# A fused FFN / attention / FFN kernel: its first pass begins on rounded weights ahead of the branch on their low parts

## The reference

```
x = x + 0.5 * ffn(layernorm(x))
x = x + attention(layernorm(x))
x = x + 0.5 * ffn(layernorm(x))

ffn(x): h = silu(lin(x, w1)) * lin(x, w2)     # 256 -> 1024
        h = gelu(lin(h, h1))                  # 1024 -> 1024
        h = gelu(lin(h, h2))                  # 1024 -> 1024
        return lin(h, w3)                     # 1024 -> 256
lin(x, w) = (x @ w.T) * scale                 # w holds -1, 0, 1 in the given inputs
```

## Time and profile before

| | us |
|---|---|
| median of 3 runs | 1589.89 (1585.19 to 1591.61) |
| profiled execution | 1588.57 |
| its span, first to last instruction | 1586.7 |
| PE busy | 1498.8 |
| DVE busy | 1085.1 |
| ACT busy | 676.7 |
| POOL busy | 553.8 |
| mean DMA rate over the span | 216 GB/s |

### The profile page before, as it was taken

One profiled execution on the slowest core, in us unless ns is written; L12 is line 12 of the kernel. 1 busy time (PEld: TensorE's weight loads), 2 busy tenths in 40 slices (PEclk: granted clock), 3 DMA queues, 4 the chain that ended last, 5 costly groups with the idle time before them and its releaser, 6 DMA issues.

```text
span 1586.7 us, 19160 instructions
## 1 busy us (share of the span) xinstructions
PE 1498.8 (94%) x6978; PEld 1222.8 (77%) x6978; DVE 1085.1 (68%) x1475; ACT 676.7 (43%) x1062; POOL 553.8 (35%) x402
## 2 busy tenths in 40 slices
PE   7689999999999999999999999999999999998998
PEld 6567888778777778787778877768788877786887
DVE  6323768895777687777876867778676978793322
ACT  7434445353343435354434353434343444352442
POOL 2003051535171607162526070533615245434020
PEclk9899999999999999999999999999999999999999
DMA  8763848666776494857765757557475776754332
GB/s 309 264 225 112 285 143 308 224 210 229 235 243 214 157 316 148 280 178 276 255 231 192 253 180 267 181 194 257 159 263 179 264 247 222 274 202 148 130 98 76
DMA packets 189218, 342.41 MB, mean 216 GB/s; under 512 B 15552, under 2 KB 138560, under 8 KB 188736
## 3 DMA queue, kind: packets, MB, share of 16 engines
q1 hardware_dynamic: 189120, 341.13, 62.7%
HBM read 319.05 MB, written 30.41 MB: 220 GB/s over the span
## 4 chain that ended last, share of the span: by engine, by line
PE 67%; DVE 11%; POOL 8%; DMA 7%; ACT 4%; issue 3%; SPq 0%; DVEq 0%; POOLq 0%; ACTq 0%
PE f_bank L1103 22%; PE f_bank L1104 22%; PE a_banks L1181 6%; PE f_bank L1032 4%; PE f_bank L1033 4%; DMA weights_hi<-in_ffn_w 4%; POOL acc L695 3%; PE f_bank L1132 2%; PE f_bank L1133 2%; DVE slot L937 2%; DVE S L943 2%; DVE slot L981 2%; PE a_banks L1201 2%; POOL acc L692 1%; POOL h_lo L709 1%
## 5 line engine op out<-in xcount | busy, mean ns | idle before, releaser
L1103 PE MATMUL f_bank<-h_hi,wring 128*128 128x512 f32 x2048 | 812.5, 397 | 35.9 <-POOL h_lo L709 13.3
L1104 PE MATMUL f_bank<-h_lo,wring 128*128 128x512 f32 x2048 | 801.7, 391 | 0.0
L1103 PEld LDWEIGHTS f_bank<-h_hi,wring 128*128 128x128 f32 x2048 | 387.1, 189 | 125.0 <-issue 21.3
L1104 PEld LDWEIGHTS f_bank<-h_lo,wring 128*128 128x128 f32 x2048 | 387.0, 189 | 80.8 <-issue 1.4
L775 ACT ACTIVATE h_hi<-f_bank,colv 128x512 fp32r<-128x512 f32 x256 | 176.2, 688 | 532.1 <-PE f_bank L1104 531.8
L897 DVE TENSOR_TENSOR h_lo<-f_bank,h_hi 128x512 fp32r<-128x512 f32 x256 | 174.7, 686 | 242.0 <-ACT f_bank L776 240.9
L709 POOL TENSOR_TENSOR h_lo<-f_gated,h_hi 128x512 fp32r<-128x512 f32 x128 | 165.8, 1308 | 442.9 <-ACT h_hi L769 442.1
L1032 PE MATMUL f_bank<-fT_hi,w_in 128*128 128x512 f32 x480 | 195.6, 408 | 13.6 <-ACT f_gated L764 6.4
L1033 PE MATMUL f_bank<-fT_lo,w_in 128*128 128x512 f32 x480 | 189.2, 394 | 0.0
L981 DVE TENSOR_TENSOR slot<-slot,a_banks 128x1280 f32<-128x1280 f32 (+4 forms) x124 | 169.4, 1375 | 20.4 <-DMA slot<-keys_and_values 20.2
L937 DVE TENSOR_TENSOR slot<-slot,a_banks 128x1280 f32<-128x1280 f32 (+4 forms) x124 | 170.5, 1375 | 18.6 <-DMA slot<-keys_and_values 18.4
(11 more groups left out here) (117 smaller groups left out, 1327.8 us busy)
## 6 DMA issues: line engine op xcount, KB each, us to landing
wring<-weights_hi SPq DMA_DIRECT2D x256, 512.0 KB, 4.7
slot<-keys_and_values SPq DMA_DIRECT2D x128, 384.0 KB, 4.7
slot<-keys_and_values SPq DMA_DIRECT2D x64, 640.0 KB, 4.0
slot<-keys_and_values SPq DMA_DIRECT2D x312, 128.0 KB, 4.5
slot<-keys_and_values SPq DMA_DIRECT2D x64, 256.0 KB, 5.5
weights_hi<-in_ffn_w SPq DMA_DIRECT2D x16, 512.0 KB, 5.1
keys_and_values<-kv_out SPq DMA_DIRECT2D x32, 256.0 KB, 2.3
xf<-in_x SPq DMA_DIRECT2D x8, 512.0 KB, 6.2
```

The source lines that it names most:

```text
L1103: pe.matmul(bank[:, :], hi, h_hi[src][:, k, :], start=(k == 0), stop=False)
L1104: last = pe.matmul(bank[:, :], hi, h_lo[src][:, k, :], start=False, stop=(not general and k == KH - 1))
```

## The change

The diff moves more of pass 0 ahead of the branch and gives new numbers to the planner.

- The input layer of pass 0 now uses the normal `f_in`, on the rounded weights in `w_in` (it waits for ACT's cut, `s_hi`) and on the rounded tile and its remainder. `first_in` is gone.
- The first inner layer of pass 0 also runs ahead of the branch. ACT writes its blocks straight into the ring: 0 to 3 as slots come, 4 to 7 when PE is done with the slot. Its steps count on semaphores of their own (`b_marks`). Blocks are looked at in a new order.
- The branch comes behind that layer. ACT and POOL now read the flag too, and where weights have low parts a repetition (`beginning(begins[1])`) does both layers again with them. The test is turned round: the version without low parts comes first, the general one is the `Else`.
- SP no longer fetches ring blocks ahead of the branch. It copies blocks 8 to 11 there; `wproj` and the zero rows (`w_proj`), and the other copies, come behind the branch, in the planner's order. The wait for the zero rows moves to their first users.
- DVE's scaling of constants (`w_scale`) moves from right behind the branch into the planner's order.
- `TIMES`, `FOLLOW`, `OPENING`, `STARTS` and the costs of PE's steps get new values.

```diff
-TIMES = [4.5, 9.5, 11.8, 13.4, 16.0, 24.8, 22, 3.8, 5.6, 53.0, 58.4, 3.1, 87.5, 3.5]
+TIMES = [4.03, 9.45, 11.2, 13.1, 17.5, 26.66, 22, 3.95, 6.75, 53.01, 60.41, 3.2, 94.86, 3.17]
-STARTS = [70, 149, 219, 312, 386, 453, 537, 617,
-          688, 768, 847, 925, 1006, 1087, 1158, 1236]
+STARTS = [41.0, 114.5, 182.4, 268.3, 337.6, 405.3, 485.5, 567.2,
+          636.9, 716.8, 782.1, 866.5, 947.5, 1023.3, 1099.1, 1163.8]
...
-    LOOK = [*range(H_BLOCKS, H_BLOCKS + IN_BLOCKS), *range(H_BLOCKS), *range(H_BLOCKS + IN_BLOCKS, BLOCKS)]
-    FETCHED = 4
-    COPY_AT, FETCH_AT = [15, 17], [19, 21]
+    LOOK = [W_IN, W_IN + 1, W_IN + 2, W_IN + 3, 0, 1, 2, 3, 8, 9, 10, 11, 12, 13, 4, 5, 14, 15, 6, W_OUT, 7, W_OUT + 1]
+    COPY_FIRST, COPY_AT = [8, 9, 10, 11], [17, 18, 20, 21]
...
+        def high(b):
+            j = LOOK[b]
+            if j >= W_OUT:
+                return w_out3[:, j - W_OUT, :]
+            if j >= W_IN:
+                return w_in[:, j - W_IN, :]
+            return wring[:, j % 4, :] if j < KH else pairs[b % 2][:, :].bitcast(fp32r)
...
-            for i in range(FETCHED, H_BLOCKS):
-                steps.append((begin["f_hidden", 0, i // KH, i % KH] - 14, "copy", (i,)))
-            steps += [(2.0, "w_max", ()), (3.0, "w_log", ()), (6.0, "w_merge", ())]
+            for i in range(H_BLOCKS):
+                if i not in COPY_FIRST:
+                    steps.append((begin["f_hidden", 0, 1, i - KH] - 14 if i >= KH else begin["f_hidden", 1, 0, i] - 40, "copy", (i,)))
+            steps += [(1.0, "w_proj", ()), (10.0, "w_scale", ()), (11.0, "w_max", ()),
+                      (12.0, "w_log", ()), (14.0, "w_merge", ())]
...
+        def beginning(r, clock):
+            steps = []
+            for m in range(KH):
+                steps.append((clock, "f_in", (r, m)))
+                clock += 1.82
+                steps += [(clock + FOLLOW[step], "f_" + step, (r, m)) for step in ("silu", "gate", "cut", "low")]
+            for m in range(KH):
+                steps.append((clock, "f_hidden", (r, 0, m)))
+                clock += [6.35, 0.91, 3.63][min(m, 2)]
+                steps += [(clock + FOLLOW[step], "f_" + step, (r, 0, m)) for step in ("gelu", "lo")]
+            return steps
...
             def freed(self, r, i):
-                if i >= self.slots:
-                    return r.at(MM, self.blocks[i - self.slots][4])
...
+                before = i - self.slots
+                j = r.j if before >= 0 else r.j - 1
+                if j < 0:
+                    return b_marks.mm, begins[0].of("mm", 3 * KH)
+                count = self.blocks[before][4]
+                if j == 0 and count <= 3 * KH:
+                    return b_marks.mm, begins[self.slots == 2].of("mm", count)
+                return f_marks.mm, passes[j].of("mm", count)
...
+            def w_proj():
+                sp.wait_ge(s_compared, BLOCKS - 1)
+                sp.dma_start(wproj[:, :, :], proj_w).then_inc(s_const, 16)
+                sp.wait_ge(s_zero, 1)
+                sp.dma_start(kv_dram[:, :, 0:PAD, :].rearrange("t b p d -> p (t b) d"),
+                             acc[:, 0:1, :].to_broadcast([P, 2 * B, D])).then_inc(s_padded, 16)
...
-            sp.wait_ge(s_padded, 16)
-            with sp.If(has_lo != 0):
+            with sp.If(has_lo == 0):
+                run(False)
+            with sp.Else():
                 lo_parts()
                 run(True)
-            with sp.Else():
-                run(False)
...
             def w_cut(b):
-                (block, semaphore, uses), j = place(b), LOOK[b] - H_BLOCKS
...
+                (block, semaphore, uses), j = place(b), LOOK[b]
+                if 4 <= j < KH:
+                    act.wait_ge(b_marks.mm, begins[0].of("mm", 2 * KH + j - 4 + 1))
+                    act.wait_ge(s_compared, LOOK.index(j - 4) + 1)
+                elif KH <= j < H_BLOCKS:
                     act.wait_ge(s_compared, b - 1)
-                else:
...
                 act.wait_ge(semaphore, 16 * uses + 16)
-                act.activation(dst, block, ACT.Copy).then_inc(s_hi, 1)
+                act.activation(high(b), block, ACT.Copy).then_inc(s_hi, 1)
...
+            act.wait_ge(s_flag, 1)
+            has_lo = act.value_load(flag[0:1, 0:1])
+            with act.If(has_lo != 0):
+                schedule({"f_silu": f_silu_, "f_cut": f_cut, "f_gelu": f_gelu_}, beginning(begins[1], 0.0))
...
+            def w_count():
+                pe.wait_ge(s_summed, 1)
+                pe.matmul(t_bank[0:1, 0:1], differ_sum[:, :], ones[:, :], start=True, stop=True).then_inc(s_counted, 1)
+
+            pe.wait_ge(s_ident, 16)
+            ring = Ring(False)
+            schedule({"f_turn": f_turn, "w_count": w_count, "f_in": lambda r, m: run_in(r, m, ring, False),
+                      "f_hidden": lambda r, layer, m: run_hidden(r, layer, m, ring, False)}, opening())
+            pe.wait_ge(s_flag, 1)
+            has_lo = pe.value_load(flag[0:1, 0:1])
...
-            with pe.If(has_lo != 0):
+            with pe.If(has_lo == 0):
+                run(False)
+            with pe.Else():
+                begin_again()
                 run(True)
-            with pe.Else():
-                run(False)
```

More of the change, by code:

```diff
@@ L12 @@
 from concourse import mybir
+from collections import namedtuple
 from contextlib import ExitStack
@@ L30 @@
          "z", "out"]
-TIMES = [4.5, 9.5, 11.8, 13.4, 16.0, 24.8, 22, 3.8, 5.6, 53.0, 58.4, 3.1, 87.5, 3.5]
-FOLLOW = dict(silu=-1.5, gate=0.1, cut=1.9, low=2.0, gelu=-0.6,
-              lo=0.9, residual=-1.3, residual2=0.4, fill=20.7, stats=-0.6, turn=4)
-OPENING = dict(block=5.2, block_step=1.8, compare=2.4, done=15.5, step=3.1, turn=8.5)
-STARTS = [70, 149, 219, 312, 386, 453, 537, 617,
-          688, 768, 847, 925, 1006, 1087, 1158, 1236]
+TIMES = [4.03, 9.45, 11.2, 13.1, 17.5, 26.66, 22, 3.95, 6.75, 53.01, 60.41, 3.2, 94.86, 3.17]
+FOLLOW = dict(silu=-1.5, gate=0.1, cut=2.12, low=2.21, gelu=-1.01,
+              lo=0.9, residual=-1.57, residual2=-0.2, fill=23.38, stats=-1.02, turn=4)
+OPENING = dict(block=6.5, block_step=1.84, compare=1.3, turn=8.7, input=13.0, count=52.85)
+STARTS = [41.0, 114.5, 182.4, 268.3, 337.6, 405.3, 485.5, 567.2,
+          636.9, 716.8, 782.1, 866.5, 947.5, 1023.3, 1099.1, 1163.8]
 class Counts:
@@ L48, in at, with __init__, of @@
         return sub.batch * self.total + self.before[sub.c] + k
+Marks = namedtuple("Marks", "mm silu prod phi low gelu lo")
 class Pass:
-    def __init__(self, j, tile, second, last):
+    def __init__(self, j, tile, second, last, marks, per, begun):
         self.j, self.p, self.tile, self.second, self.last = j, j % 2, tile, second, last
+        self.marks, self.per, self.begun = marks, per, begun
     def at(self, per_pass, k):
         return self.j * per_pass + k
+    def of(self, what, k):
+        return self.j * self.per[what] + k - self.begun[what]
+class Begin:
+    def __init__(self, attempt, marks, per):
+        self.attempt, self.marks, self.per = attempt, marks, per
+        self.j = self.p = 0
+        self.last = False
+    def at(self, per_pass, k):
+        return k
+    def of(self, what, k):
+        return self.attempt * self.per[what] + k
 class Sub:
@@ L310, in macaron_kernel @@
         order += [(t, True) for t in range(4, TILES)]
-        passes = [Pass(j, tile, second, j == 2 * TILES - 1) for j, (tile, second) in enumerate(order)]
+        per_pass, per_begin = dict(mm=MM, input=KH, lo=LO), dict(mm=3 * KH, input=KH, lo=KH)
+        passes = [Pass(j, tile, second, j == 2 * TILES - 1, f_marks, per_pass, per_begin)
+                  for j, (tile, second) in enumerate(order)]
+        begins = [Begin(attempt, b_marks, per_begin) for attempt in range(2)]
         first_pass = {r.tile: r for r in passes if not r.second}
@@ L420, in opening @@
                 steps += [(here, "w_cut", (b,)), (here + at["compare"], "w_compare", (b,))]
[L421 to L425, removed]
+            steps += [(here + at["compare"] + 0.1, "w_sum", ()), (at["count"], "w_count", ()), (at["count"] + 0.5, "w_flag", ())]
+            return [*steps, *beginning(begins[0], at["input"])]
         def schedule(do, steps):
@@ L635, in fill @@
                     source, blk, _, _, _ = ring.blocks[i]
[L636 to L639, removed]
+                    after(sp, *ring.freed(r, i))
+                    if r.j < 2 and not general:
                         sp.wait_ge(s_copied[blk], 16)
@@ new lines, in w_flag, with f_lo_ @@
+            def w_flag():
+                dve.wait_ge(s_counted, 1)
+                dve.tensor_scalar(flag[:, :], t_bank[0:1, 0:1], 1.0, None, ALU.min).then_inc(s_flag, 1)
+            def f_lo_(r, layer, m):
+                bank = f_bank(r, hidden_use(layer, m))
+                i = (r.p + 1 + layer) % 2
+                dve.wait_ge(r.marks.gelu, r.of("lo", layer * KH + m + 1))
+                dve.tensor_tensor(h_lo[i][:, m, :], bank[:, :], h_hi[i][:, m, :].bitcast(fp32),
```

(13 more changed lines are left out.)

220 lines of the change are left out of this document (95 added, 125 removed).

## The result

The changed kernel takes 1548.03 us, median of 4 runs (1546.01 to 1552.32), against 1588.59 (1585.19 to 1591.61, 4 runs): ratio 0.9744, 95% interval 0.9726 to 0.9762. Its profiled execution took 1546.01 us with a span of 1544.1, so the two spans differ by 42.6 us.

A forecast was written before the change was run, and what follows sets the result against it. PE's work plus its pauses bound the kernel. Pass 0 was to end at 104.2 us against 137.7, 33.5 sooner, with 0 behind it: 1588.6 - 33.5 = 1555, forecast 1556, range 1541 to 1578 (main case 0.60, 1545 to 1568).

The forecast's parts named there:

- Input layer: Pass 0's opening: starts at 13.7 us, 64 rounded matmuls take 14.5 plus 2.4 for cold start, ends at 30.6.
- Hidden layer 0 ahead of the branch: Pass 0: starts at 30.6, ends at 59, ring waits cost nothing; 29 us go from the critical path.
- Flag: DVE's compares in pass 0: flag at 56, 6 us later than before but 3 us before PE is done.
- Branch: Behind the flag: SP needs 3 us, first fill issued at 59, landed 3.5 later, layer 1 starts at 63.
- Late fills: Ring fills in layer 1 of pass 0, block 12 onward: late by 0 to 8 us, taken as 3.
- w_scale behind wproj: DVE step in pass 0 now waits for wproj, landing at 13 to 15; PE wants it at 18.2: costs nothing.
- Pass 0: End of pass 0's output layer: 104.2 us against 137.7, 33.5 us sooner.
- Everything behind: Passes after pass 0: same PE instructions, counted as 0 us, with bounds of 10 us either way.
- (a): Stretch behind the flag stays slow: SP 8 us, restart 2.4, fills late by 8; 1566 or 1572; chance 0.16.
- (b): Behind pass 0: new places also close later pauses, ten us more, 1545; chance 0.12.
- (c): Attention: shorter sub-tile period, DVE cannot follow and PE waits 44 us against 33.5 gained; 1600; chance 0.06.
- (d): Gain is swallowed: pass 0 ends early but attention holds the end as before; 1588; chance 0.06.

The follow-up runs named there:

- fp32 run: Changed kernel with pass 0's input layer ahead of the branch in fp32 again, one 512-column matmul replacing two rounded ones: 1561.11 us against 1550.25 on the same chip.
- old kernel with the new places: Kernel before, opening and branch untouched, with the new planner numbers behind the branch (TIMES, FOLLOW, PE step costs, STARTS plus 29.04): 1586.14 us, ratio 0.996.
- run with the early copies: Changed kernel with the DRAM copies of blocks 12 to 15 issued ahead of the flag: 1551.21 us, ratio 0.9752 to the kernel before.

## Why the prediction was right

1556 was forecast, 1548 measured; the way is that of its main case, and so is most of the size (34 of 41 us).

- *Input layer.* Start 13.7, measured 13.89; end 30.6, measured 29.84. That a length of 13 us there counts in full at the end of pass 0 was an argument, and the fp32 run shows it.
- *Hidden layer 0 ahead of the branch.* End 59, measured 59.9. The cuts of blocks 4 to 7 never made PE wait. This is the largest term, 29 us, and it is read from the two timelines; no run puts the layer back behind the branch by itself.
- *Flag.* 56, measured 56.1, behind PE's last block but one, as said.
- *Branch: the term that was mis-sized.* 3 us for SP; it took 0.85. The row of the old jump was taken as the nearest, and it was a row of another thing. First fill 56.94 and not 59, layer 1 at 60.30 and not 63, and no cold restart: 3.5 us of the 8 that were missed. The rule of the Trainium skill that was weighed against the row (Runtime: NRT & Kernel Launch, Instruction fetch mechanics) had SP go on near 56.5 and layer 1 near 60, and the runs agree with it: 3.4 us with the jump and 0.85 without on SP, 8.0 and 1.0 on PE.
- *Late fills.* 3 us, measured 3.1 (40.5 for 37.4). The size was right for a cause that was half right: the copy of block 12 took 8.0 us beside wproj and the zero rows, and behind it ACT's table loads stood ready to cost much of it again.
- *w_scale behind wproj.* Costed at nothing; right. The danger was its neighbour w_log, which the prediction didn't look at.
- *Pass 0.* 33.5 us sooner, measured 36.9.
- *Everything behind.* 0 with 10 either way, measured 5.7 in the two profiles, some 3 over all profiles and 5 to 6 by the medians. The count of collisions (ten in both) says too little: PE's waits for POOL went from 13.3 us to 0.3, while those of the input layer for DVE went from 5.8 to 12.5 and those of attention's projections for ACT from 2.1 to 8.0. The places exchange one wait for others, and the pauses fall by 2 us in all. Which step meets the input layer may count more than how many do; no run shows that.

Of the rivals, (a) is ruled out by PE's 0.4 us pause. (b) is partly what happened. (c) would have shown in the old kernel with the new places, which got faster: DVE has the slack. (d) falls with the result: pass 0 ends 36.9 us sooner and the span ends 42.6 sooner.

What stays open: why the new places are better, by how much within 3 to 6 us, and how the 39 us behind the branch would split if the layer and the order of the copies were changed one at a time.

## What to carry to other kernels

Work that needn't know a flag belongs ahead of the test, as far as the engine that sets the pace has time for it; the gain is that engine's time, and here what followed took over the end of that stretch nearly one for one (13.6 us at the handover, 11 in the medians). Put the case that runs directly behind the test, on the engine that others wait for first of all. Where two delays lie side by side, take both away before you judge either, and judge a few microseconds at the handover in the trace rather than in the total.

## What the runs showed of the hardware

The same instructions behind the same pauses of PE met another clock. In the changed kernel, at 262 us, twelve projection matmuls behind pauses of 2.01 and 0.97 us:

```profile
262.00:275.00 13.00, 11.23 (x48) 7.99 (x49) 6.45 (x9) 4.79 (x9) 11.64 (x7) 1.00 0.56 185
...
264.43 3.71 PE L1222 MATMUL a_banks<-wproj,aT 128*128 128x512 f32 x12 [0.97 <-ACT aT L829]
```

In the run with the early copies, behind the same two pauses:

```profile
262.00:275.00 13.00, 11.57 (x37) 7.84 (x38) 5.10 (x7) 2.82 (x6) 11.61 (x7) 0.74 0.39 136
...
264.09 6.59 PE L1224 MATMUL a_banks<-wproj,aT 128*128 128x512 f32 x12 [0.97 <-ACT aT L831]
```

At clock 1.00 they took 3.7 us, with 0.74 over the stretch (a part at 1.2 GHz, the rest at 2.4) 6.6. The changed kernel's own second profile has 0.74 there and took 6.3 us for the twelve, behind pauses of 2.01 and 0.69. That is 2.6 of the 3.7 us by which its stretch behind the handover is the longer one, and so a part of why the first pair of profiles shows 5.7 us and all of them 3. It isn't the whole spread: the run with SP's test turned back has 0.74 there as well and only 1444.8 us behind the handover, the old kernel with the new places has 1.00 and 1446.8.
